# The round of an attention loop put in another order, with idle transposes ahead of it

## The reference

```python
q, k, v = einsum(x, Wq), einsum(x, Wk), einsum(x, Wv)       # 32 query heads, 8 key heads, D = 128
q, k = rope(rmsnorm(q, q_norm_w), pos), rope(rmsnorm(k, k_norm_w), pos)
k_all = concatenate([k_cache[block_table], k]); v_all = concatenate([v_cache[block_table], v])   # 512 + 128 keys
scores = where(valid, einsum(q, k_all) * SCALE, -1e30)
o = einsum(softmax(scores), v_all)
x = x + einsum(o, Wo)                                       # then a dense layer, a gated one with adapters, a third
```

## Time and profile before

| | us |
|---|---|
| median of three runs | 1397.55 |
| the profiled execution | 1396.84 |
| its span, first to last instruction | 1395.0 |
| TensorE busy | 1359.6 (97%) |
| VectorE busy | 1005.3 (72%) |
| ScalarE busy | 847.7 (61%) |
| GpSimd busy | 676.0 (48%) |

### The profile page before, as it was taken

How to read it: one execution, slowest core, us unless ns; L and a number is a source line. 1 busy time by engine, 2 the same in 40 slices (tenths; PEclk the granted TensorE clock), 3 DMA queues, 4 the chain that set the end, 5 groups by cost and what they waited for, 6 DMA issues and landing times. The chain is left out here.

```text
span 1395.0 us, 25230 instructions
## 1 busy us (share of the span) xinstructions
PE 1359.6 (97%) x7752; PEld 1184.2 (85%) x7752; DVE 1005.3 (72%) x2102; ACT 847.7 (61%) x2212; POOL 676.0 (48%) x968
## 2 busy tenths in 40 slices
PE   5999999999999999999999999999999899999999
PEld 4888888888888888888888888888888677888887
DVE  6777777777777778777877787777777787756544
ACT  6665666666566667666666666556666476535444
POOL 6765465456545555655565555555644222311202
PEclk9999999999999999999999999999999999999999
DMA  5345225423642364146315621573210264354523
GB/s 186 106 167 166 61 77 163 140 61 90 192 102 67 91 209 106 30 123 205 78 30 150 195 60 30 150 210 91 61 31 16 65 221 140 121 154 162 178 98 113
DMA packets 161995, 163.92 MB, mean 118 GB/s; under 512 B 121488, under 2 KB 129296, under 8 KB 151568
## 3 DMA queue, kind: packets, MB, share of 16 engines
q1 hardware_dynamic: 156144, 128.06, 31.5%
q0 software_dynamic: 5792, 35.13, 7.7%
HBM read 131.71 MB, written 31.46 MB: 117 GB/s over the span
## 5 line engine op out<-in xcount | busy, mean ns | idle before, releaser
L517 ACT ACTIVATE at_pT_hi<-at_ps 128x512 fp32r<-128x512 f32 x320 | 178.4, 600 | 173.5 <-PE at_ps L912 173.2
L432 POOL TENSOR_SCALAR at_probs<-at_probs,at_row_inv 128x640 f32<-128x640 f32 x256 | 205.4, 803 | 153.2 <-DVE at_row_inv L737 145.0
L682 DVE TENSOR_TENSOR at_pT_lo<-at_ps,at_pT_hi 128x512 fp32r<-128x512 f32 x320 | 208.1, 683 | 91.7 <-ACT at_pT_hi L517 91.7
L731 DVE CUSTOM_DVE_ANT_0 at_scores<-at_ps,at_mask,at_inv_rms 128x640 f32<-128x640 f32 x256 | 224.1, 878 | 66.0 <-PE at_ps L65 63.8
L560 ACT ACTIVATE at_probs<-at_scores,at_neg_max 128x640 f32<-128x640 f32 x256 | 213.1, 833 | 58.5 <-DVE at_neg_max L731 57.0
L63 PE MATMUL at_ps<-at_kT_hi,at_qT_hi 128*128 128x320 f32 x512 | 164.6, 322 | 0.3 <-DVE at_qT_lo L682 0.2
L912 PE MATMUL at_ps<-ident,at_probs 128*128 128x128 f32 x1280 | 160.6, 272 | 1.7 <-POOL at_probs L432 1.7
L64 PE MATMUL at_ps<-at_kT_lo,at_qT_hi 128*128 128x320 f32 x512 | 158.1, 309 | 0.0
L65 PE MATMUL at_ps<-at_kT_hi,at_qT_lo 128*128 128x320 f32 x512 | 158.1, 309 | 0.0
L912 PEld LDWEIGHTS at_ps<-ident,at_probs 128*128 128x128 f32 x1280 | 145.2, 140 | 10.6 <-POOL at_probs L432 2.4
L63 PE MATMUL at_ps<-at_pT_hi,at_v_hi 128*128 128x512 f32 x320 | 131.7, 412 | 2.1 <-DVE at_pT_lo L682 2.1
(11 more groups left out here) (214 smaller groups left out, 3447.0 us busy)
## 6 DMA issues: line engine op xcount, KB each, us to landing
kT_pages<-shared SPq DMA_DIRECT2D x14, 1024.0 KB, 4.6
v_pages<-shared SPq DMA_DIRECT2D x14, 1024.0 KB, 4.6
at_k_raw<-kT_pages SPq DMA_DIRECT2D x56, 256.0 KB, 3.5
at_v_raw<-v_pages SPq DMA_DIRECT2D x56, 256.0 KB, 4.0
sw_wgu_raw<-in_sw_gu SPq DMA_DIRECT2D x22, 512.0 KB, 3.4
staging<-in_L_cond_Wq SPq DMA_DIRECT2D x8, 1024.0 KB, 6.8
staging<-in_L_cond_Wo SPq DMA_DIRECT2D x8, 1024.0 KB, 5.4
shared<-in_mask_Bx4096x_ik SPq DMA_DIRECT2D x7, 1024.0 KB, 5.5
```

Of the source, the lines that this page charges most:

```text
L432: pool.tensor_scalar(probs[:, h, :], probs[:, h, :], row_inv[:, h:h + 1], 1.0, ALU.mult, ALU.mult).then_inc(probs_done, 1)
L517: act.activation(out, src, ACT.Copy).then_inc(done, 1)
L682: dve.tensor_tensor(out, src, hi_part.bitcast(F32), ALU.subtract).then_inc(done, 1)
L731: dve.tensor_tensor_reduce(out=scores[h % 2][:], in0=slot(h), in1=mask[:, b, :], scale=inv_rms[b % 2][:, h:h + 1], scalar=3.0e38, op0=ALU. ...
```

## The change

TensorE's round now begins with the turns, all in one run: chunks 0 and 1 of the probabilities of batch b, the queries and the new keys of the next batch, chunks 2 to 4. Then come values 0 and 1, the whole projection of the queries two ahead, scores 0 and 1 of the next batch, values 2 and 3, score 2, values 4, score 3, the keys and values three ahead, and the output of this same batch b. The other engines' lists are rewritten to it. The rotation of keys and queries is two batches ahead, and `new_kv` is taken apart into `turn_k` and `new_values`. The bank of `times_v`'s result and that of the output alternate with the batch, and so do two halves of the bank of keys and values; the sign `y_bank_free` goes, since VectorE's own order now gives it. Wq's halves are made in rounds 5 and 6, Wk's and Wv's in rounds 4 and 5, Wo's low halves half by GpSimd and half by VectorE. The first scores, maxima and normalisations stand ahead of the first round. The last group's mask weights of the dense layer are made in more of its rounds. Ahead of everything TensorE does 74 turns of the identity into bank 0, whose result is not used.

The diff's core (of the lists of ScalarE and VectorE only the new one is shown; the label ahead of a list names its engine):

```diff
-        Q_BANK, KV_BANK, O_BANK, Y_BANK = 4, 5, 6, 7
-        PROBS_BANK = [0, 1, 2, 3, 0]
-        KC_BANK = 3
+        Q_BANK, KV_BANK, KC_BANK = 4, 5, 3
+
+        def o_bank(b):
+            return 7 - b % 2
+
+        def y_bank(b):
+            return 6 + b % 2
+
+        def probs_bank(b, c):
+            return [0, 1, 2, y_bank(b), 3][c]
+
+        def kv_half(b, at, cols):
+
+            at += KV_BANK * NFREE + (b % 2) * 2 * D
+            return ps[:, at:at + cols]
+
+        def project_kv_at(g, b, at, cols):
+
+            if isinstance(g, int) and g == 0 and b == 1:
+                return ps[:, y_bank(0) * NFREE + at:y_bank(0) * NFREE + at + cols]
+            return kv_half(b, at, cols)
...
-        KV_GROUPS, WO_GROUPS = DC // 2, G
+        KV_GROUPS, WO_GROUPS, WARM = DC // 2, G, 74
...
     gpsimd:
             query_scale(0, 0)
+            key_scale(0, 1)
             rotate_q(0, 1)
+            for h in range(G):
+                normalise(0, 0, h)
+            rotate_k(0, 1)
+            query_scale(0, 1)
...
+                    if more2:
+                        key_scale(g2, b2)
+                    if b == B - 3 and not last:
                         qkv_group(g + 1, DC)
                         qkv_group(g + 1, DC + 1)
                     if more2:
+                        rotate_k(g2, b2)
+                    if b == 0:
+                        wo_group(g, 0)
+                        wo_group(g, 1)
+                    if not last and 1 <= b < 5:
+                        stage_pages(g, b - 1)
+                    if more2:
                         rotate_q(g2, b2)
-                    if b == 0:
-                        wo_group(g, 3)
+                    if more:
+                        for h in range(G):
+                            normalise(g1, b1, h)
+                    if more2:
+                        query_scale(g2, b2)
...
     scalar:
+            tokens(2)
+            key_squares(0, 1)
+            new_values(0, 1)
             squares(0, 1)
+            for h in range(G):
+                exps(0, 0, h)
+            key_squares(0, 2)
+            for b in range(2):
+                cached_values(0, b)
+            cached_keys(0, 1)
...
+                    probs_T(g, b, 0)
+                    probs_T(g, b, 1)
                     if more:
                         queries(g1, b1)
+                        new_keys(g1, b1)
+                    for c in range(2, KC):
+                        probs_T(g, b, c)
+                    if b == 0:
+                        for n in range(WO_GROUPS):
+                            wo_group(g, n)
+                    if by_row(g) and b < B - 3:
+                        tokens(b + 3)
+                    if b == B - 3 and not last:
+                        qkv_group(g + 1, 0)
+                        qkv_group(g + 1, 1)
+                    if more2:
+                        squares(g2, b2)
                     if more:
+                        exps(g1, b1, 0)
+                        exps(g1, b1, 1)
+                    hi(oT_hi[:], bank(o_bank(b)), pv_done, upto(g, b, KC, KC), oT_hi_done)
                     if more:
+                        exps(g1, b1, 2)
+                        exps(g1, b1, 3)
+                    if more3:
+                        key_squares(*following(g2, b2))
                     if more2:
+                        new_values(g2, b2)
+                        cached_values(g2, b2)
+                        cached_keys(g2, b2)
+                    if b == B - 4 and not last:
+                        qkv_group(g + 1, DC)
+                        qkv_group(g + 1, DC + 1)
+                    if b == B - 3 and not last:
+                        qkv_group(g + 1, 2)
+                        qkv_group(g + 1, 3)
...
     vector:
+            mask_and_max(0, 0, 0)
+            mask_and_max(0, 0, 1)
+            inverse(0, 0, 0)
+            mask_and_max(0, 0, 2)
+            inverse(0, 0, 1)
+            mask_and_max(0, 0, 3)
+            new_values(0, 1)
+            turn_k(0, 1)
+            inverse(0, 0, 2)
+            inverse(0, 0, 3)
+            for b in range(2):
+                cached_values(0, b)
+            cached_keys(0, 1)
...
+                    if b == B - 2 and not last:
+                        qkv_group(g + 1, 2)
+                    probs_T(g, b, 0)
+                    probs_T(g, b, 1)
                     if more:
                         queries(g1, b1)
+                        new_keys(g1, b1)
+                    probs_T(g, b, 2)
                     if first and b < B - 2:
                         table(b + 2)
+                    if b == B - 2 and not last:
+                        qkv_group(g + 1, 3)
+                    for c in range(3, KC):
+                        probs_T(g, b, c)
+                    if last and b == B - 1:
+                        dense.weights(dve, 1, 2)
+                    if more2:
+                        turn_k(g2, b2)
+                    if b == 0:
+                        wo_group(g, 2)
+                    if first and b < B - 3:
+                        tokens(b + 3)
+                    if more2:
+                        turn_q(g2, b2, 0)
+                        turn_q(g2, b2, 1)
                     if more:
+                        mask_and_max(g1, b1, 0)
+                        mask_and_max(g1, b1, 1)
+                        inverse(g1, b1, 0)
+                    if b == 0:
+                        wo_group(g, 3)
+                    if b == B - 3 and not last:
+                        qkv_group(g + 1, 0)
                     if more:
+                        mask_and_max(g1, b1, 2)
+                        inverse(g1, b1, 1)
+                    attended(g, b)
                     if more:
+                        mask_and_max(g1, b1, 3)
+                        inverse(g1, b1, 2)
+                        inverse(g1, b1, 3)
+                    if b == B - 3 and not last:
+                        qkv_group(g + 1, 1)
                     if more2:
+                        new_values(g2, b2)
+                        cached_values(g2, b2)
+                    if more2 and not by_row(g2):
+                        cached_keys(g2, b2)
                     if last:
+                        for at, c in {B - 4: ((0, 0), (0, 1)), B - 3: ((0, 2), (0, 3)), B - 2: ((1, 0), (1, 1)),
+                                      B - 1: ((1, 3), (2, 0), (2, 1), (2, 2))}.get(b, ()):
+                            dense.weights(dve, at, c)
+                    add_y(g, b)
+                    if more2 and by_row(g2):
+                        cached_keys(g2, b2)
...
     tensor:
+            for _ in range(WARM):
+                pe.transpose(bank(0)[:, 0:P], ident[:], ident[:])
...
+            project_kv(0, 1)
+            for h in range(G):
+                score(0, 0, h)
+            project_kv(0, 2)
 
             def group(g, first, last):
                 for b in range(B):
                     g1, b1 = following(g, b)
-                    more, more2 = not (last and b == B - 1), not (last and b >= B - 2)
-
-                    def project_ahead(cs):
-                        if more2:
-                            project_q(*following(g1, b1), cs)
-
-                    score(g, b, 0)
-                    score(g, b, 1)
-                    if more:
-                        queries(g1, b1)
-                    score(g, b, 2)
-                    score(g, b, 3)
-                    if not (first and b == 0):
-                        output(g, b, range(G))
-                    if more:
-                        project_kv(g1, b1)
+                    g2, b2 = following(g1, b1)
+                    more, more2, more3 = (not (last and b >= B - n) for n in (1, 2, 3))
+
                     if more and by_row(g1):
                         pe.wait_ge(scores_done, upto(g, b, G, G))
                         cached_keys(g1, b1)
-                    for c in range(3):
+                    probs_T(g, b, 0)
+                    probs_T(g, b, 1)
+                    if more:
+                        queries(g1, b1)
+                        new_keys(g1, b1)
+                    for c in range(2, KC):
                         probs_T(g, b, c)
-                    project_ahead(range(2))
-                    times_v(g, b, 0, first)
-                    times_v(g, b, 1, first)
-                    probs_T(g, b, 3)
-                    probs_T(g, b, 4)
-                    project_ahead(range(2, 3))
-                    times_v(g, b, 2, first)
-                    project_ahead(range(3, 4))
+                    times_v(g, b, 0)
+                    times_v(g, b, 1)
+                    if more2:
+                        project_q(g2, b2, range(DC))
                     if more:
-                        new_keys(g1, b1)
-                    times_v(g, b, 3, first)
-                    times_v(g, b, 4, first)
+                        score(g1, b1, 0)
```

(44 more changed lines are left out.)

199 lines of the change are left out of this document (67 added, 132 removed).

## The result

| | before | after |
|---|---|---|
| median of five runs, us | 1396.98 | 1389.81 |
| lowest to highest | 1395.79 to 1397.94 | 1388.70 to 1391.66 |
| the profiled execution's span | 1395.0 | 1388.8 |
| TensorE busy | 1359.6 | 1357.7 |

What follows compares the result with a forecast made beforehand. TensorE's own stream was taken to set the round; gains of 1.9 + 1.7 + 2.0 + 5.1 + 4.1 = 14.8 us off 1396.84 gave 1382.0, with 0.7 for the median 1382.7 us. The range was 1376 to 1399.

Steps and rivals of the forecast that it cites:

- What bounds the kernel: TensorE's own instruction stream sets a round's time; what attention saves is passed on one to one.
- Part 1: Ordinary rounds: one run of turns instead of four, round 16.87 to 16.775 us, 5.1 us gained in 54 rounds.
- The turns' formula: TensorE's 128x128 transposes: a run of n costs about 0.03 + (n-1) x 0.109 us, so 2.65 for 25.
- The restarts: The first matmul behind each run of turns lasts 0.08 us longer; four a round before, one after.
- Part 2: Ordinary round: every result is ready when TensorE needs it, tight slacks 0.7, 0.8 and 0.64 us; reordering costs nothing.
- Rival B: Score 3's chain to the next turns ends late; slower from 0.9 us over the layout, 1419 at 1.2; chance 0.08.
- Part 3: Start: 74 turns raise the clock, so the first turns over probabilities start at 31.6, not 33.54 us: 1.9 gained.
- Round 0 and the next six: First group's rounds: round 0 from 19.1 to 17.4 us, 1.7 gained; the next six 105.24 to 103.2, 2.0 gained.
- Part 4: End of attention, from round 5's turns to the last output: 43.5 to 39.4 us, 4.1 gained.
- A: The clock takes the long run of turns as idle time and falls in most rounds: about 1473 us; chance 0.08.
- C: Start's turns don't raise the clock, merged run harmless: 5 us of gain lost, 1388; chance 0.16 together with D.
- D: Turns gain nothing in the round, restart cost returns between scores and values: 1388 us; chance 0.16 together with C.

Runs made afterwards that it cites:

- e5: The kernel before with VectorE's loop over groups 1 to 6 written out: 1395.22 us, ratio 0.9982.
- e1: The changed kernel with VectorE's loop over groups 1 to 6 written out, the other engines' loops kept: 1381.32 us, ratio 0.9890.
- e3: The changed kernel without the 74 idle turns at the start: 1392.52 us, ratio 0.9966.
- e6: e1's kernel with the turns of chunks 3 and 4 moved behind values 0 and 1, so two runs of turns a round: 1411.63 us, ratio 1.0100.
- e9: The changed kernel with ScalarE's zeros of the second adapter rows written two loop steps later in the gated layer: 1387.30 us, ratio 0.9925.
- e8: e1's kernel with the last group's dense weights of rounds 4 to 6 moved behind turn_k and inverse 0: 1380.39 us, ratio 0.9877.
- e4: The kernel before, in its old order, with the 74 idle turns put ahead of everything: 1407.64 us, ratio 1.0074.
- e7: e4's kernel with TensorE's loop over groups 1 to 6 written out: 1397.27 us, ratio 0.9995.
- e2: The changed kernel with TensorE's loop over groups 1 to 6 written out, VectorE's kept: 1389.23 us, ratio 0.9942.
- e10: e8's kernel with ScalarE's zeros of the second adapter rows written two loop steps later: 1377.58 us, ratio 0.9858.

## Why the prediction was half right

**What bounds the kernel** held: TensorE's stream sets the round, and what attention saves is passed on, but for 2 us.

**Part 1, too small.** The turns' formula held (2.65 us for 25). The restarts were a little undersized, and a term was missing. The forecast gave four of 0.08 against one, 0.24 us, less 0.17 for the turns themselves. Measured, an ordinary round fell from 16.84 to 16.67, 0.17 us instead of 0.08. By e5 0.05 of this is what VectorE's loop cost the old order in each round, so the order itself saves 0.12, and the restarts that it saves come to 0.12 + 0.17 = 0.29. Most of it can be seen in the projection, which took 2.94 in three pieces (1.47 from 614.62, 0.78 from 618.26, 0.69 from 619.75) and takes 2.75 in one. Round 6 of each group gains more, 0.34 (17.00 in e5, 16.66 in e1). Over the 54 rounds the new order is worth 908.07 - 900.29 = 7.8 us instead of 5.1, and being free of the cost of VectorE's looped code 2.9 more: 10.6 together, as e1 shows.

**Part 2, the step that failed.** "I cost all of it at nothing" was true of the instructions and left out the loop's branch back. Its layout of an ordinary round held to a few hundredths: chunk 0's low half at 1.95 us (forecast 1.94); GpSimd's last normalisation ends at 623.49 + 0.80 = 624.29, where the next run starts at 624.94 (slack 0.65, forecast 0.64). Rival B, which lives from these slacks, didn't occur. But the new order put the end of VectorE's pass between the residual's addition and chunk 0's low half. That is the place with the slack of 0.7, and the branch back, which stalls VectorE for 3 us now, makes the low half 2.3 us late there. Five such passes at 1.5 to 1.7 and a few tenths of smaller waits make the 8.4 us of e1. The rows of before couldn't give this price, since there the same branch took 0.3 us. The prediction's own slacks gave the warning: none was over 0.8 us, so anything that the profile doesn't list and that takes longer had to show.

**Part 3** held. The turns end at 11.28 (forecast 11.7), the first turns over probabilities start at 31.70 (31.6). e3 shows the mechanism, not only the sum; that the start came out to 0.1 us is in part luck, since with the same turns e6 and e9 start 1.3 and 2.3 us later. Round 0 and the next six fell 0.3 and 0.4 us short of it; one of the six took 18.0 us, the others 17.1 to 17.2, and why was not tried.

**Part 4, too large by 3.** Two costs were left out. The dense layer's weights, moved ahead of the low halves, made values 0 of round 6 wait 0.71 us; e8 takes 1.46 us off that round (15.57 to 14.11) and 0.4 off round 5. And where no keys are projected any more, the 1.43 us that lay between score 3 and the output are gone, and with them the cover of attended's low half: TensorE then waits for it. The rows of the changed kernel in rounds 5 and 6:

```profile
1075.24 0.50 PE L63 MATMUL at_ps<-at_woT_hi,at_oT_hi 128*128 128x512 f32 x1 [0.53 <-DVE at_oT_lo L710]
...
1081.76 0.51 PE L63 MATMUL at_ps<-at_pT_hi,at_v_hi 128*128 128x512 f32 x1 [0.71 <-DVE at_pT_lo L710]
...
1090.45 0.50 PE L63 MATMUL at_ps<-at_woT_hi,at_oT_hi 128*128 128x512 f32 x1 [0.53 <-DVE at_oT_lo L710]
```

The working subtracted the projection's 1.42 from the round in full, though by its own layout the low half came at 13.1, only 0.6 behind score 3's end. e8 left both waits of 0.53 as they were. The weights' 1.9 us and these 1.06 are the 3 us.

**Behind attention** the forecast had nothing. The clock fall at 1154.84 cost about 1.6 us in the profiled execution, and 0.3 more had been lost by the end of the dense part. The falls hide how much the dense part lost: before had two of them there, that of the earlier trace rows and the one in this window, and after has none, and still the dense part gained nothing.

```profile
1130.70:1134.10 3.40, 3.40 (x11) 2.53 (x9) 3.40 (x8) 3.17 (x8) 0.10 (x1) 0.50 0.77 263
```

TensorE waits up to 1.23 us for VectorE in the same stretch after; what limits it there wasn't tried by itself.

**The rivals.** A is refuted: the granted clock was 1.00 through every run of 25 turns. The Trainium skill, "TensorE: Matmul & The Clock Gate", Part 4, says that transposes do not count as activity for the clock; here 74 of them alone raised it, and without them (e3) it rose only at 18 us, behind the first matmuls. C falls with it. D is half answered: the turns' merging gains by itself, but e6 shows that more than its borders' price hangs on it, since the run also covers the halves.

## What to carry to other kernels

A change to a loop's instructions, or only to how many stand ahead of it, can make an engine's branch back over ten times as long (VectorE 0.3 to 3.1 us, TensorE 0.2 to 3.8). So look at the branch's own records in the new kernel, and at what stands behind it: the same 3 us or more cost 1.6 us a pass in the changed kernel, 1.9 to 3.7 in e4, and nothing in e3, where the engine waited there anyway. An idle time at a loop's end that the profile puts down to a releaser long done is the sign of it; writing out that engine's loop is a cheap test, one engine at a time. And when work is dropped from a late round, what lay under it becomes a wait: subtract it from the round only after looking at what it covered.

## What the runs showed of the hardware

A branch back of a loop is either short or long, and which of the two it is goes with the kernel, not with the engine or the pass. VectorE's list stands still for 0.25 to 0.29 us behind it before, in e4 and in e7, and for 2.9 to 3.2 us after, in e2, e3 and e9. TensorE's lasts 0.2 us before, after, and in e1, e5, e6, e8, e9 and e10, but 3.3 to 3.8 in e4 and 3.3 to 3.6 in e3. From before to e4, 74 turns more ahead of the loop made it long; from after to e3, 74 fewer did. Neither the busy time nor the timeline shows it. What decides between the two was not tried. The granted clock falls to 0.50 for 3.4 us or for 6.8 us and comes back by itself. In e4 it fell once inside attention as well, at 850 us, in a pass whose branch made TensorE wait. The start also varies by itself: the same 74 turns took 9.75 us in the changed kernel's execution and 11.24 in e9's.
